# Two PSUM banks for the scores and three for the maxima in the second layer's attention, in place of three and two

## The chip, the cores and the metric

The kernel runs on one core of one Trainium2 chip. The metric is the device time of one execution in microseconds (us). Three runs of the kernel before took 1433.34, 1433.45 and 1435.84 us; their median is 1433.45 us.

## What is computed

Eight sequences of 512 tokens with 256 features go through two layers. The first is attention with 16 heads of 16 features, with rotary positions and q and k scaled to unit length. The second is an ordinary attention, without those two, followed by a mixture of eight experts, of which each token goes to the one with the largest gate. Cut to what matters here:

```python
# first layer, per sequence
q, k = unit(rope(q)), unit(rope(k))
attn = softmax(q @ k.T / 4)
x = layernorm(x + (attn @ v) @ Wo + bo)
# second layer
h = layernorm(x) * ln1_w + ln1_b
q, k, v = split(h @ w_qkv)
y = x + (softmax(q @ k.T / 4) @ v) @ w_proj
out = layernorm(x + y + expert_of_token(layernorm(y) * ln2_w + ln2_b))
```

In the first layer the scores can't exceed a small number, since q and k have unit length, so no maximum is taken off before the exponential. In the second layer they can, and each row's maximum has to be known before the exponential is taken.

## The kernel before, in words

There are 16 passes of attention: 0 to 7 for the first layer's eight sequences, 8 to 15 for the second layer's. They run as a pipeline. In one stage the scores of pass b are computed (it is the *attended* pass), while the next pass is *projected* (q, k and v) and the one before it *finished* (output projection, norms, routing). A stage has 16 quads of four chunks. A chunk is one head and one tile of 128 keys: its scores for all 512 queries fill one PSUM bank. "3.1" stands for chunk 1 of quad 3 of a stage. A stage is called by its attended pass.

TensorE (PE) issues everything in an order written out in the source: for every chunk the score matmul (`score`, L450), then, in the second layer, one max tile (`max_score`, L482), after chunk 1 of the quad the four value products of an earlier quad (`pv`, L467), and then whatever the tables PROJECTED, ATTENDED and FINISHED place at that chunk (`task`). L511 are projections of q and k, L525 those of v, L555 the output projection, L533, L548, L501 and L563 transposes, L540 the transposition of the negated maxima.

A max tile is the same product of q and k with the queries on the partitions: 128 queries of one head by 512 keys. VectorE (DVE) takes the maximum of each row, negated (`max_tile`, L868). When a group of four heads has its 16 tiles, `neg_split` (L873) splits the negated maxima into three bf16 parts; PE transposes them (L540), ScalarE (ACT) copies them (L727) and issues a DMA (L732) that puts them as three more rows into the stack of q. The score matmul of the second layer thus subtracts the maximum by itself: it has 99 rows in place of 96. The max tiles run six quads ahead of the scores (MAX_LEAD = 6): from quad 10 of a stage they are those of the next pass. So maxima appear from quad 10 of pass 7 to quad 9 of pass 15.

ACT takes the exponential of each chunk (`exp`, L665), in order, and between chunks does its own tasks of the tables: L688 copies projections to bf16, L681 copies transposed inputs, L674 the finished value products, L741 and L713 other copies, L749 and L753 the reciprocal deviation of a norm, for which it waits for DVE's moments (L968, L972). DMAs issued by ACT stand in its order too.

PSUM has eight banks of 128 x 512 fp32. Bank 4 is for projections, bank 5 (in the first layer also bank 7) for outputs, bank 6 for value products. In passes 0 to 6 the scores have banks 0 to 3. From pass 7 on, before the change, they have banks 0 to 2, and the max tiles banks 3 and 7. Two rules keep these apart. `st_bank` (L362) gives a score its bank and the count of exponentials that must be done before it may be written; with three banks that is the exponential of three chunks earlier. `mx_ring` (L348 to L360) counts, for each max bank, the reduces that have read it; `max_score` waits until its bank's last use has been reduced, with two banks that of two tiles earlier.

```python
wait(pe, exps, read)                       # score: the bank has been read
wait(pe, *mx_ring.free(b, (g, c)))         # max_score: the bank has been reduced
```

Of the kernel before, what the change touches and what calls it, by code (L numbers as in the profile page):

```python
# [25 lines left out]
CHUNKS = QUADS * HEADS_AT_ONCE  # L26
# [23 lines left out]
LAST_A = BATCH - 1  # L50
# [98 lines left out]
def program(nc, x, w_qkv1, w_o1, b_o, ln1_w, ln1_b, w_qkv2, w_o2, ln2_w, ln2_b, gate_w, gate_b,  # L149
# [5 lines left out]
    with ctx:  # L155
# [22 lines left out]
        psum = [ctx.enter_context(nc.psum_tensor(f"bank{i}", [P, T], FP32)) for i in range(8)]  # L178
# [163 lines left out]
        N_FIRST, N_LATER, N_CONST_OPS = 7, 12, 4  # L342


        st_banks, mx_banks, pv_bank = psum[0:4], (psum[3], psum[7]), psum[6]
        p_ring = Ring("proj", [psum[4]], sem)
        o_ring = Ring("out", [psum[5], psum[7]], sem)
        mx_ring = Ring("max", mx_banks, sem)  # L348
# [8 lines left out]
        for b in range(BATCH, 2 * BATCH):  # L357
            for g in range(GROUPS):
                for c in range(HEADS_AT_ONCE * TT):
                    mx_ring.add(b, (g, c), c % 2)  # L360

        def st_bank(b, c):  # L362

            if b < LAST_A:
                return st_banks[c % 4], CHUNKS * b + c - 3
            return st_banks[(CHUNKS * (b - LAST_A) + c) % 3], CHUNKS * b + c - 2

        def tiles(ap, b):
            return ap[b].rearrange("(t p) d -> p t d", p=P)
# [64 lines left out]
        def _(pe):  # L434
# [3 lines left out]
            def score(b, c):  # L438

                q, j = c // HEADS_AT_ONCE, c % HEADS_AT_ONCE  # L440
                g, kt = q // TT, q % TT
                rows = STACK + (NEG if second(b) else 0)
                if c == 0:
                    for arrived in stack_in:
                        pe.wait_ge(arrived, 16 * STACK_DMAS * (b + 1))
                if second(b) and j == 0 and kt == 0:
                    pe.wait_ge(neg_in, 16 * GROUPS * (b - BATCH) + 16 * (g + 1))
                bank, read = st_bank(b, c)
                wait(pe, exps, read)
                nc.tensor.matmul(bank[:, :],  # L450
                                 k_stack[0:rows, b % 2, HEADS_AT_ONCE * g + j,
                                         kt * P:(kt + 1) * P],
                                 q_stack[0:rows, b % 2, HEADS_AT_ONCE * g + j, :],
                                 start=True, stop=True).then_inc(scores, 1)
# [202 lines left out]
        def _(act):  # L657
            nc.scalar.preload_act_table_set("natural_log_exp_and_others")

            def exp(b, c):  # L660
                q, j = c // HEADS_AT_ONCE, c % HEADS_AT_ONCE
                act.wait_ge(scores, CHUNKS * b + (c + 1))
                if j == 0:
                    wait(act, pv_done, QUADS * b + q + 1 - PROBS)
                nc.scalar.activation(probs[:, q % PROBS, j, :], st_bank(b, c)[0][:, :],  # L665
                                     ACT.Exp, scale=SCALE).then_inc(exps, 1)
# [178 lines left out]
        def _(dve):  # L845
# [27 lines left out]
            def neg_split(b, g):  # L873

                last_tile = HEADS_AT_ONCE * TT - 1
                dve.wait_ge(*mx_ring.empty(b, (g, last_tile - 1)))
                dve.wait_ge(*mx_ring.empty(b, (g, last_tile)))
                if g:
                    dve.wait_ge(*o_ring.full(b, f"NG{g - 1}"))
                elif b > BATCH:  # L880
                    dve.wait_ge(*o_ring.full(b - 1, f"NG{GROUPS - 1}"))
                n = 3 * GROUPS * (b - BATCH)
                ve.tensor_copy(neg_parts[:, :, 0, :], negm[:, :, :]).then_inc(neg_step, 1)
                dve.wait_ge(neg_step, n + (3 * g + 1))
                ve.tensor_tensor(neg_rest[:, :, :], negm[:, :, :], neg_parts[:, :, 0, :],
                                 ALU.subtract).then_inc(neg_step, 1)
                dve.wait_ge(neg_step, n + (3 * g + 2))
                ve.tensor_copy(neg_parts[:, :, 1, :], neg_rest[:, :, :]).then_inc(neg_step, 1)
                dve.wait_ge(neg_step, n + (3 * g + 3))
                ve.tensor_tensor(neg_parts[:, :, 2, :], neg_rest[:, :, :], neg_parts[:, :, 1, :],  # L890
                                 ALU.subtract).then_inc(neg_ready, 1)
# [188 lines left out]
            for n in range(-1, STAGES + 1):  # L1080
                if n == 1:
                    dve.wait_ge(later_in, 16 * N_LATER)
                    ve.tensor_copy(earlier_bf[:, :], route_c[:, 0:P])
                    ve.tensor_copy(next_row[:, :], room_c)
                    ve.tensor_copy(token[:, :], tok_c)
                    dve.wait_ge(padded, 16 * (E + 1))
                for q in range(QUADS):
                    for b, g in split_group(n, q):
                        neg_split(b, g)
                    largest = max_tiles(n, q)  # L1090
                    for j in range(HEADS_AT_ONCE):
                        for tile in largest[j:j + 1]:
                            max_tile(*tile)
                        for name, b in tasks(n, q, j, DVE_LAG):
                            task(name, b)
# [300 lines left out]
```

## Time and profile before

| what | value |
|---|---|
| time, median of three runs | 1433.45 us |
| time of the profiled execution | 1429.04 us |
| its span, first to last instruction | 1427.1 us |
| PE matmuls busy | 90% of the span |
| DVE, ACT, GpSimd busy | 55%, 64%, 22% |
| mean granted TensorE clock | 0.966 |

Matmuls are pipelined and their ends are modelled, so a busy PE is not a PE at its peak; the distance between the starts of two matmuls tells more. "PEld" is the load of weights into PE, which can run ahead of the matmul before it. In a timeline a row has its start, its length, engine, line and operation, what it writes and reads, how many of them follow one another (x5), and in brackets the idle time of the engine before it and what ended that. Instructions on ACT and DVE overlap a little at their ends. "ACTq" is a DMA issued by ACT.

### The profile page before, as it was taken

How to read it: one execution, taken by the hardware profiler on the slowest of the kernel's cores; microseconds unless marked ns; L12 is line 12 of the kernel's file. 1: busy time of each engine (PE TensorE's matmuls, PEld its weight loads, DVE VectorE, ACT ScalarE, POOL GpSimd, SP SyncE). 2: the span in 40 equal slices, each digit the busy share in tenths (PEclk: the TensorE clock that was granted, in tenths of full speed). 3: DMA queues.
4: the chain of work that ended last, by engine and by line, in shares of the span. 5: the costliest groups of instructions: out<-in, count | busy, mean ns of one | idle time of the engine just before them, and what ended most of it. 6: DMA issues, size and time to landing. Idle time of an engine off the chain costs nothing. (4 is left out here: it accounts for less than half of the span.)

```text
span 1427.1 us, 21029 instructions
## 1 busy us (share of the span) xinstructions
PE 1279.5 (90%) x7238; PEld 687.5 (48%) x7238; DVE 792.0 (55%) x1815; ACT 919.6 (64%) x1617; POOL 311.5 (22%) x247
## 2 busy tenths in 40 slices
PE   3599999999999898999999999999961899999993
PEld 1233443443443333444434443444331898989993
DVE  3333554554552677787878787878823333433341
ACT  0277777777777565676666666766640477767773
POOL 5122233233232110222222222212122011111111
PEclk9799999999999999999999999999995899999997
DMA  7231331331432121214131313131357111111113
GB/s 194 88 99 46 127 114 56 127 114 55 127 114 92 57 90 60 81 54 104 46 104 47 105 46 109 51 96 61 134 183 244 53 49 53 56 54 52 52 56 133
DMA packets 103496, 127.87 MB, mean 90 GB/s; under 512 B 7168, under 2 KB 91008, under 8 KB 103264
## 3 DMA queue, kind: packets, MB, share of 16 engines
q1 hardware_dynamic: 71088, 79.06, 17.6%
q10 hardware_dynamic: 27872, 33.95, 7.5%
q0 software_dynamic: 4432, 13.52, 3.1%
q8 instruction: 60, 0.98, 0.3%
q14 instruction: 44, 0.36, 0.1%
HBM read 51.51 MB, written 28.46 MB: 56 GB/s over the span
## 5 line engine op out<-in xcount | busy, mean ns | idle before, releaser
L665 ACT ACTIVATE w_space<-bank 128x512 f32<-128x512 f32 x1024 | 564.4, 601 | 288.3 <-PE bank L450 275.4
L868 DVE TENSOR_REDUCE negm<-bank 128x1 f32<-128x512 f32 x512 | 334.3, 685 | 97.2 <-PE bank L482 93.6
L450 PE MATMUL bank<-w_space 96*128 96x512 bf16 (+1 forms) x1024 | 354.7, 385 | 12.4 <-DMA w_space<-work_space 9.8
L467 PE MATMUL bank<-w_space 128*32 128x512 f32 x2048 | 275.2, 610 | 0.6 <-ACT w_space L674 0.6
L450 PEld LDWEIGHTS bank<-w_space 96*128 96x128 bf16 (+1 forms) x1024 | 93.6, 99 | 278.2 <-ACT w_space L665 204.3
L482 PE MATMUL bank<-w_space 96*128 96x512 bf16 x512 | 197.3, 385 | 16.4 <-DVE negm L868 7.6
L638 PE MATMUL bank<-w_space,work_space 128*128 x624 | 141.4, 380 | 0.0
L511 PE MATMUL bank<-work_space,wqkv_sb 128*128 128x512 f32 x256 | 123.0, 603 | 7.5 <-DVE w_space L995 4.8
L638 PEld LDWEIGHTS bank<-w_space,work_space 128*128 128x128 f32 x624 | 115.5, 190 | 14.2
L1222 POOL TENSOR_TENSOR work_space<-w_space,work_space 128x1024 bf16<-128x1024 f32 x32 | 68.3, 2136 | 226.1 <-ACT work_space L713 145.7
L1278 POOL DMA_INDIRECT out_rows<-rows_sb,work_space x39 | 37.5, 963 | 267.6 <-DVE rows_sb L1172 267.6
L482 PEld LDWEIGHTS bank<-w_space 96*128 96x128 bf16 x512 | 50.1, 98 | 90.9 <-DVE negm L868 50.2
L467 PEld LDWEIGHTS bank<-w_space 128*32 128x32 f32 x2048 | 40.6, 108 | 99.5 <-issue 75.7
L1256 POOL TENSOR_TENSOR row_sb<-row_sb,rows_sb 128x512 f32<-128x512 f32 x32 | 38.0, 1187 | 207.8 <-DVE row_sb L976 207.8
L625 PEld LDWEIGHTS bank<-work_space 128*128 128x128 f32 x640 | 76.5, 196 | 1.9 <-DVE work_space L1145 0.9
L625 PE MATMUL bank<-work_space 128*128 128x128 f32 x640 | 76.8, 279 | 0.5 <-DVE work_space L1145 0.5
L1158 DVE TENSOR_TENSOR wqkv_sb<-bank,work_space 128x256 f32<-128x256 f32 x39 | 16.6, 425 | 104.7 <-PE bank L638 104.7
L511 PEld LDWEIGHTS bank<-work_space,wqkv_sb 128*128 128x128 f32 x256 | 48.2, 192 | 49.4 <-issue 31.4
L625 PEld LDWEIGHTS bank<-work_space,wqkv_sb 128*128 128x128 f32 x608 | 70.8, 192 | 1.7 <-DVE work_space L1145 0.8
L625 PE MATMUL bank<-work_space,wqkv_sb 128*128 128x128 f32 x608 | 71.1, 275 | 0.5 <-DVE work_space L1145 0.5
L525 PE MATMUL bank<-wqkv_sb,work_space 128*128 128x256 f32 x256 | 62.5, 388 | 2.5 <-DVE w_space L1008 1.7
L555 PE MATMUL bank<-wo_sb,w_space 128*128 128x256 f32 x256 | 60.8, 380 | 2.5 <-ACT w_space L741 1.6
(131 smaller groups left out, 1451.5 us busy)
## 6 DMA issues: line engine op xcount, KB each, us to landing
w_space<-work_space SPq DMA_DIRECT2D x384, 128.0 KB
w_space<-in_w_dram ACTq DMA_DIRECT2D x16, 1024.0 KB, 8.5
work_space<-rows_dram SPq DMA_DIRECT2D x39, 256.5 KB, 2.6
work_space<-in_x_dram ACTq DMA_DIRECT2D x16, 512.0 KB, 3.8
x_dram<-xo SPq DMA_DIRECT2D x16, 256.0 KB, 3.2
h_dram<-row_sb SPq DMA_DIRECT2D x16, 256.0 KB, 2.2
work_space<-h_dram ACTq DMA_DIRECT2D x8, 512.0 KB, 3.9
work_space<-x_dram ACTq DMA_DIRECT2D x8, 512.0 KB
```

The lines of the kernel that those rows point to most:

```text
L450: nc.tensor.matmul(bank[:, :], k_stack[0:rows, b % 2, HEADS_AT_ONCE * g + j, kt * P:(kt + 1) * P], q_stack[0:rows, b % 2, HEADS_AT_ONCE * ...
L467: last = nc.tensor.matmul(pv_bank[VW * j:VW * (j + 1), :], v_aug[:, b % 2, at:at + VW], probs[:, q % PROBS, j, :], start=(kt == 0), stop=( ...
L482: nc.tensor.matmul(mx_ring.bank(b, (g, c))[:, :], q_stack[0:STACK, b % 2, h, qt * P:(qt + 1) * P], k_stack[0:STACK, b % 2, h, :], start=Tr ...
L511: last = nc.tensor.matmul(bank[:, :], wqkv_sb[:, second(b), k, c * P:(c + 1) * P], xT[:, k, :], start=(k == 0), stop=(k == KD - 1))
L525: last = nc.tensor.matmul(bank[:, j * D:(j + 1) * D], xT[:, k, tt * P:(tt + 1) * P], wqkv_sb[:, second(b), k, 2 * D:3 * D], start=(k == 0) ...
L555: last = nc.tensor.matmul(bank[:, t * D:(t + 1) * D], onT[:, u, t, k, :], wo_sb[:, second(b), k, :], start=(k == 0), stop=(k == KD - 1))
L625: last = nc.tensor.matmul(psum[2 * (j % 2) + n][:, f * P:(f + 1) * P], w1_tile[j % 2][:, k, at:at + P], xsT[:, j % 2, k, :], start=(k == 0 ...
L638: last = nc.tensor.matmul(psum[5 + j % 2][:, 0:D], hidT[:, j % 2, k, :], w2_sb[:, bass.ds(e, 1), k, :].rearrange("p a d -> p (a d)"), star ...
L665: nc.scalar.activation(probs[:, q % PROBS, j, :], st_bank(b, c)[0][:, :], ACT.Exp, scale=SCALE).then_inc(exps, 1)
L868: ve.tensor_reduce(negm[:, c % TT, c // TT:c // TT + 1], mx_ring.bank(b, (g, c))[:, :], axis=AX.X, op=ALU.max, negate=True).then_inc(mx_ri ...
L1222: pool.tensor_tensor(parts[:, qk, 2, :, :], rest[:, qk, :, :], parts[:, qk, 1, :, :], ALU.subtract).then_inc(parts_ready, 1)
L1256: pool.tensor_tensor(both, both, rows_sb[:, r:r + 1, :].to_broadcast([P, 2, D]), ALU.mult).then_inc(hw_step, 1)
```

## The change

From pass 7 on, the scores alternate between banks 0 and 1, and a score waits for the exponential of two chunks earlier. Bank 2 goes to the max tiles, which take banks 2, 3 and 7 in turn through all passes; a max tile waits for the reduce of three tiles earlier. Before the negated maxima of a group are split, DVE waits for the last use of each of the three banks in place of two.

```diff
-        st_banks, mx_banks, pv_bank = psum[0:4], (psum[3], psum[7]), psum[6]
+        st_banks, mx_banks, pv_bank = psum[0:4], (psum[2], psum[3], psum[7]), psum[6]
...
-                    mx_ring.add(b, (g, c), c % 2)
+                    mx_ring.add(b, (g, c), len(mx_ring.uses) % len(mx_banks))
...
-            return st_banks[(CHUNKS * (b - LAST_A) + c) % 3], CHUNKS * b + c - 2
+            return st_banks[c % 2], CHUNKS * b + c - 1
...
-                dve.wait_ge(*mx_ring.empty(b, (g, last_tile - 1)))
-                dve.wait_ge(*mx_ring.empty(b, (g, last_tile)))
+                for back in range(len(mx_banks)):
+                    dve.wait_ge(*mx_ring.empty(b, (g, last_tile - back)))
```

## Rows read from the trace of the kernel before

**Rows 1.** The page: span, and busy time of each engine.
```profile
span 1427.1 us, 21029 instructions
PE 1279.5 (90%) x7238; PEld 687.5 (48%) x7238; DVE 792.0 (55%) x1815; ACT 919.6 (64%) x1617; POOL 311.5 (22%) x247
```

**Rows 2.** Stretches (passes 7, 8, 9-14, 15): length, busy us (count) per engine, clock, DMA.
```profile
434.29:502.96 68.67, 58.84 (x302) 22.61 (x300) 29.43 (x70) 44.44 (x87) 11.81 (x8) 0.98 0.25 79
502.96:579.51 76.55, 71.23 (x354) 27.49 (x352) 56.41 (x123) 46.34 (x89) 11.35 (x7) 0.93 0.22 70
579.51:994.41 414.90, 407.72 (x2281) 179.14 (x2278) 329.46 (x738) 279.79 (x527) 90.75 (x79) 1.00 0.24 74
994.41:1051.20 56.79, 52.58 (x313) 19.87 (x311) 37.15 (x93) 39.16 (x77) 11.55 (x12) 1.00 0.40 140
```

**Rows 3.** Waits in passes 9 to 14: who waited for whom: total us, times, longest.
```profile
PEld bank L450 <- ACT w_space L665: 61.8, 78, 0.8
...
PEld bank L482 <- DVE negm L868: 25.6, 61, 0.7
```

**Rows 4.** Timelines of PE and ACT in pass 12, around chunk 3.1.
```profile
800.67 0.38 PE L482 MATMUL bank<-w_space 96*128 96x512 bf16 x1
800.89 0.38 PE L450 MATMUL bank<-w_space 99*128 99x512 bf16 x1
801.40 0.39 PE L482 MATMUL bank<-w_space 96*128 96x512 bf16 x1
...
800.73 0.73 ACTq L732 DMA_DIRECT2D w_space<-neg_T  x1
801.56 0.60 ACT L688 ACTIVATE work_space<-bank 128x512 bf16<-128x512 f32 x1 [0.86 <-ACT neg_T L727]
...
802.05 2.56 ACT L665 ACTIVATE w_space<-bank 128x512 f32<-128x512 f32 x5
```

**Rows 5.** The same timelines, around chunk 8.3.
```profile
826.39 0.38 PE L450 MATMUL bank<-w_space 99*128 99x512 bf16 x1
...
826.87 0.30 ACT L749 ACTIVATE rstd<-mv,eps_sb 128x4 f32<-128x4 f32 x1 [1.28 <-DVE mv L972]
...
827.31 2.76 ACT L665 ACTIVATE w_space<-bank 128x512 f32<-128x512 f32 x5
```

**Rows 6.** The same timelines, around chunk 15.1.
```profile
852.66 0.38 PE L450 MATMUL bank<-w_space 99*128 99x512 bf16 x1
853.04 0.39 PE L482 MATMUL bank<-w_space 96*128 96x512 bf16 x1
...
853.07 0.60 ACT L665 ACTIVATE w_space<-bank 128x512 f32<-128x512 f32 x1 [0.81 <-PE bank L450]
```

**Rows 7.** The same timelines, around chunk 7.0.
```profile
818.65 0.38 PE L450 MATMUL bank<-w_space 99*128 99x512 bf16 x1
819.16 0.39 PE L482 MATMUL bank<-w_space 96*128 96x512 bf16 x1
...
818.52 1.57 ACT L665 ACTIVATE w_space<-bank 128x512 f32<-128x512 f32 x3 [0.81 <-PE bank L450]
```

**Rows 8.** Timeline of PE in passes 7 and 12: two waits of other tasks.
```profile
455.29 1.98 PE L511 MATMUL bank<-work_space,wqkv_sb 128*128 128x512 f32 x4 [1.31 <-DVE w_space L1000]
...
850.45 0.39 PE L540 MATMUL bank<-ident_bf,neg_parts 128*12 128x128 bf16 x4 [0.44 <-DVE logits L1069]
```

**Rows 9.** Timelines of PE and DVE in pass 8, quads 13 and 14.
```profile
565.16 0.61 PE L482 MATMUL bank<-w_space 96*128 96x512 bf16 x1 [1.69 <-DVE negm L868]
...
568.64 0.69 DVE L868 TENSOR_REDUCE negm<-bank 128x1 f32<-128x512 f32 x1 [2.14 <-PE bank L482]
...
574.44 0.69 DVE L868 TENSOR_REDUCE negm<-bank 128x1 f32<-128x512 f32 x1 [1.51 <-PE bank L482]
```

**Rows 10.** A stretch of pass 8 (as rows 2), and PE's timeline in pass 7.
```profile
564.45:574.69 10.24, 9.53 (x34) 2.79 (x35) 6.12 (x16) 3.73 (x9) 2.21 (x2) 0.50 0.07 24
...
473.08 0.38 PE L482 MATMUL bank<-w_space 96*128 96x512 bf16 x1 [2.48 <-issue]
```

## Prediction

> **What bounds the kernel now.** I read the page first: TensorE (PE) is busy for 1279.5 of 1427.1 us [rows 1]. Its first wave, the first layer, keeps four score banks, so only passes 7 to 15 can change. The table of stretches cuts these out. The six passes 9 to 14 take 414.90 us, 69.15 each, and PE is busy for 407.72 of them at granted clock 1.00, while VectorE (DVE) has 329.46 and ScalarE (ACT) 279.79 [rows 2]. So PE sets the pace there, and a pass grows by what PE stands still, whoever causes it. The next view is the waits of these six passes. PE's weight loads wait 61 times, 25.6 us in all, for DVE to give back a bank for the maxima, and 78 times, 61.8 us, for an exponential (exp) [rows 3]. A reader must take these sums with care: a load runs ahead of the matmul before it, so part of such a wait is covered by that matmul. Hence the timeline, by starts of matmuls: score and max of one chunk are 0.22 us apart when nothing waits (800.67 to 800.89 [rows 4]); more than that is standstill. I write 3.1 for chunk 1 of quad 3 in the pass that runs from 787.14 to 856.12, one of the six; the places recur in each.
>
> **The change, part by part.**
>
> *Third max bank.* max(m) now waits for the reduce of m-3, not of m-2. The typical wait it removes is at 7.0: score at 818.65, max at 819.16 [rows 7], 0.51 apart where 0.22 would do, so 0.29 us. With 61 waits in six passes, ten a pass [rows 3], the gain is at most 10 x 0.29 = 2.9 us a pass, and nothing at least, if the score ahead of the max is late anyway.
>
> *Two score banks.* score(c) now waits until exp(c-2) has read its bank, not exp(c-3). This costs wherever ACT is busy with something else between two exps. Scores that begin today before exp(c-2) has ended stand in a few places of a pass; four of them carry nearly all of it.
>
> At 3.1 ACT first spends 0.73 us issuing the DMA of the negated maxima (from 800.73), then copies a projection (801.56), and only then runs five exps from 802.05 in 2.56 us [rows 4]. One exp is 0.60 us [rows 6]. The first of the five is exp(2.3), which ends at 802.65; score 3.1 starts at 800.89 today, so it moves by 1.76. The max behind it starts at 801.40, 0.29 later than it need; that goes. Net: **+1.47**.
>
> At 8.3 ACT sits 1.28 us for the moments (idle time in front of its row at 826.87), and exp(8.1) is the first of the five from 827.31, over at 827.91. Score 8.3 starts at 826.39 [rows 5]. Net: **+1.52**; its max waits for nothing today.
>
> At 15.1 exp(14.3) runs from 853.07 to 853.67, after another DMA issue for negated maxima; the score starts at 852.66 and its max at 853.04, 0.16 over the pace [rows 6]. Net 1.01 - 0.16 = **+0.85**.
>
> At 7.0 exp(6.2) is the first of three from 818.52, over at 819.12, and the score starts at 818.65: 0.47, less the 0.29 of its max [rows 7]. Net: **+0.18**.
>
> Quads 1, 10 and 13 are of the kind of 7.0 with a smaller lateness; I take them together at zero, the middle between losing the 0.18 of 7.0 and gaining the 0.29 of a max, each.
>
> Sum: 1.47 + 1.52 + 0.85 + 0.18 = 4.02 us a pass, **24 us in six**.
>
> Behind the waiting score stand, in PE's order, its max, the four value products of the quad and all later scores. ACT is not starved while PE waits: at 3.1 it still has exp(3.0), and exp(3.1) comes when the score is done. DVE gets its maxima later and idles. Is the delay given back later in the pass? Only where PE stands for DVE or ACT for a reason that the delay doesn't move. Pass 7 has such a place: a projection at 455.29 waits 1.31 us for DVE [rows 8] and would swallow the delay ahead of it. In the six passes the one that I find is the transposition of negated maxima at 850.45, PE idle 0.44 [rows 8]; and DVE's work ahead of it starts from PE's own maxima, so it moves along. I give nothing back.
>
> *Passes 7, 8 and 15.* Here both signs occur. In pass 8 DVE falls behind on the first layer's leftovers; a max waits until 565.16 with PE idle 1.69, after which PE runs at granted clock 0.50 (1.2 GHz) for 10.24 us, and DVE itself then runs dry for 2.14 us (before 568.64) and 1.51 us (before 574.44) [rows 9, 10]. A third bank lets PE run ahead there, so DVE needn't run dry: about 3.6 us gained, at most. Pass 7 has the same pattern, and where it has no maxima yet, late scores besides. Pass 15 has no projections but late scores to its end. Their bounds: three times the loss of a full pass, +12, and the 3.6 of pass 8 and about as much less in pass 7, -6. I take **0** for the three.
>
> *The negated maxima.* neg_split has three waits for maxima in place of two, on DVE's own reduces, of which the last still ends last: nothing, 32 waits in all.
>
> The profiled execution took 1429.04 us: 1429 + 24 = 1453. The median of the runs shown is 1433.45, 4.4 above it, so I put the forecast at 1433.45 + 24, **1457.5 us**.
>
> **The rivals.**
>
> *The clock falls.* The new standstills, 1.8 us at 3.1 and 1.5 at 8.3, come in every pass. In pass 8 PE stood 1.69 us and ran at half rate next [rows 9, 10]; such a stretch of 10.24 us costs about half of itself, 5.1 us. One in each of the six passes would add 31 us, one of a third of that length 10: 1468 to 1489, say 1480. Against it: PE stood 2.48 us before 473.08 [rows 10], and the passes 9 to 14 and that stretch show no fall. In pass 8 there were also several shorter stops just ahead. The Trainium skill, page "TensorE: Matmul & The Clock Gate", section "A second HAM failure mode: psum-queue depth-cycling", says that a TensorE which idles briefly between groups of matmuls as it cycles through PSUM banks swings between half and full clock; by that rule this rival would be the likeliest. The six passes do cycle banks with short waits at clock 1.00 [rows 2, 3], so the trace so far does not bear it out. Chance 0.15.
>
> *The third max bank wins (faster).* If the score's delay lies beside other waits, as 1.48 us could at 455.29 [rows 8], what is left is the gain on maxima: 6 x 2.9 and the 6 of passes 7 and 8, some 23 us: 1410; with half of it, 1422. It decides as soon as less of a pass's late scores reaches the end of the pass than the maxima give back. For it: the 25.6 us of waits [rows 3]. Against it: at 3.1 and 8.3 PE's work goes straight on behind the score, with no wait to lie beside. Chance 0.05.
>
> *Nothing changes.* If the exps in question were in truth over before their scores are due, or ACT's order shifted with PE's so that lateness and gain cancel, the time stays at 1433, within 3. Against it: ACT's busy stretches at 3.1 and 8.3 hang on DVE's moments and the DMA issue, not on the score. Chance 0.05.
>
> **How the numbers follow.** The forecast has 0.75. Its own ends: 6 x 3.15 (quads 1, 10 and 13 each gaining 0.29) with the edges at -6, that is +13, 1446; and 6 x 4.5 (each losing 0.18) with the edges at +12, that is +39, 1473. I reach a little into the clock's case, to 1478. Left out are most of that case and the two others, about 0.2. A measurement tells about 0.2%, 2.9 us, from no change. Faster 0.05, within 0.05, slower 0.90.
>
> **What would show it.** Right: a full pass of 73 us in place of 69.15; in each, PE idle about 1.8 us ahead of score 3.1 and 1.5 us ahead of 8.3, ended by an exp; the loads' waits for DVE's reduces near zero, those for exps well above 61.8 us; in pass 8 DVE no longer dry before 568.64 and no half clock there. Wrong: PE's idle time ahead of 3.1 unchanged; passes of 69 us or less; granted clock under 1.00 in passes 9 to 14; or a pass that grows by more than 4.5 us at clock 1.00, which would mean that ACT's own work moves behind the late scores and makes the next ones late too.

## The result, and the profile after

The changed kernel takes 1461.53 us (median of four runs, 1458.98 to 1463.29) against 1433.39 us before (four runs): slower by a ratio of 1.0188, 95% interval 1.0169 to 1.0206. The forecast was 1457.5, in a range of 1446 to 1478. The profiled execution after took 1458.98 us, 29.9 above that of before. The page's first part [rows 1]:

```profile
span 1456.9 us, 21060 instructions
...
PE 1285.8 (88%) x7238; PEld 685.7 (47%) x7238; DVE 794.9 (55%) x1815; ACT 927.1 (64%) x1617; POOL 310.9 (21%) x247
```

Every engine has the same number of these instructions as before; the 31 more in the total (21060 after 21029) are of the kinds that don't count as busy, such as waits. PE's busy time grew by 6.3 us, the span by 29.8: the loss is mostly PE standing still.

Where the time went is read from the same stretches as before, cut at the first score of each pass [rows 2]. The columns are start and end, length, busy us (and instructions) of PE, PEld, DVE, ACT and GpSimd, granted clock, DMA share and GB/s. The lines are passes 7, 8, 9 to 14 together, and of these passes 10 and 11 alone.

```profile
434.08:504.60 70.52, 61.60 (x303) 23.23 (x301) 29.42 (x70) 45.41 (x87) 11.75 (x8) 0.95 0.23 75
504.60:577.82 73.22, 67.61 (x354) 26.08 (x352) 57.20 (x123) 46.78 (x89) 11.32 (x7) 1.00 0.23 73
577.82:1022.33 444.51, 414.68 (x2281) 178.22 (x2279) 331.44 (x738) 284.90 (x527) 90.56 (x79) 0.98 0.23 69
650.91:725.64 74.73, 69.80 (x383) 30.26 (x381) 55.31 (x124) 47.61 (x89) 15.90 (x15) 0.98 0.27 72
725.64:798.73 73.09, 68.16 (x383) 29.61 (x381) 55.32 (x124) 47.61 (x89) 15.74 (x15) 1.00 0.24 73
```

Passes 9 to 14 take 444.51 us in place of 414.90, that is 29.6 more, practically the whole loss. Two of them (9 and 11) take 73.09 at granted clock 1.00, 3.94 more than the 69.15 of before. The other four take 74.3 to 74.7, each with 3.4 us at half clock. So about 6 x 3.94 = 23.6 us are standstill, and the remaining 6.0 came with the clock. The edges have both signs, as argued: pass 7 has 1.85 more, pass 8 has 3.33 less, and pass 15, from its first to its last score, takes 60.15 in place of 56.42, 3.73 more. The rest of the program has 1.9 less (29.9 - 29.6 - 1.85 + 3.33 - 3.73).

The waits of passes 9 to 14 changed places [rows 3]:

```profile
PEld bank L450 <- ACT w_space L665: 106.6, 124, 2.1
PEld bank L450 <- issue: 17.6, 33, 1.7
PEld bank L482 <- issue: 8.0, 24, 0.3
```

The 61 waits of the max loads for a reduce, 25.6 us, are gone altogether: this view has no row for them any more. The waits of the score loads for an exp rose from 61.8 to 106.6, and the longest from 0.8 to 2.1. The four places in pass 11, from the timeline of PE, each behind the matmul just before it, and (last three lines) of ACT:

```profile
738.95 0.38 PE L482 MATMUL bank<-w_space 96*128 96x512 bf16 x1
740.98 0.39 PE L450 MATMUL bank<-w_space 99*128 99x512 bf16 x1 [1.65 <-ACT w_space L665]
...
758.23 0.38 PE L482 MATMUL bank<-w_space 96*128 96x512 bf16 x1
758.97 0.39 PE L450 MATMUL bank<-w_space 99*128 99x512 bf16 x1 [0.37 <-ACT w_space L665]
...
766.18 0.38 PE L482 MATMUL bank<-w_space 96*128 96x512 bf16 x1
767.97 0.39 PE L450 MATMUL bank<-w_space 99*128 99x512 bf16 x1 [1.41 <-ACT w_space L665]
...
794.28 0.24 PE L580 MATMUL bank<-one_hot,ones_bf 128*128 128x32 bf16 x4
795.44 0.39 PE L450 MATMUL bank<-w_space 99*128 99x512 bf16 x1 [0.92 <-ACT w_space L665]
...
739.01 0.73 ACTq L732 DMA_DIRECT2D w_space<-neg_T  x1
739.84 0.60 ACT L688 ACTIVATE work_space<-bank 128x512 bf16<-128x512 f32 x1 [0.86 <-ACT neg_T L727]
740.33 1.67 ACT L665 ACTIVATE w_space<-bank 128x512 f32<-128x512 f32 x3
```

These are scores 3.1, 7.0, 8.3 and, behind four small matmuls, 15.1 [rows 4 to 7]. ACT's order at 3.1 is the old one: 0.73 us of issuing, a copy, then the exps. The first of the three, exp(2.3), ends 0.60 after 740.33; the score starts 0.05 later. By starts of matmuls, score 3.1 comes 2.03 after the max before it, 8.3 comes 1.79 after, where 0.22 would do. "Idle" in brackets is less than that, since the modelled end of the matmul before is later than the next one could start.

The half clock, in pass 10, is at the same place. The first three lines are of PE's timeline, the last of the stretches:

```profile
666.25 0.39 PE L450 MATMUL bank<-w_space 99*128 99x512 bf16 x1 [1.65 <-ACT w_space L665]
666.48 0.38 PE L482 MATMUL bank<-w_space 96*128 96x512 bf16 x1
666.79 1.57 PE L467 MATMUL bank<-w_space 128*32 128x512 f32 x8
...
667.22:670.63 3.41, 3.41 (x16) 1.53 (x9) 1.66 (x3) 0.66 (x2) 0.00 (x0) 0.50 0.71 249
```

PE stands 1.65 us ahead of score 3.1, and 0.97 us after it starts again (666.25 to 667.22) the clock falls to 1.2 GHz. In the other three passes the fall begins between 0.1 us before and 0.8 us after the start of score 3.1. The value products take 1.57 in place of 1.06. In pass 11 the same 1.65 us were followed by full clock.

In pass 8 the third bank did what was expected. DVE's row that answers to the dry spell before 568.64 [rows 9] is

```profile
567.23 3.05 DVE L868 TENSOR_REDUCE negm<-bank 128x1 f32<-128x512 f32 x5
```

Five reduces in a row, no dry spell (none from there to 575 either), and pass 8 has granted clock 1.00 where it had 0.93.

### The profile page after: what moved, and what is told of

Its sections match the earlier page's. It is cut to its first block, busy times and chain, and to the rows that moved or that the text cites. A ratio compares the mean times of both kernels' runs of the same rounds, so it can differ in the third digit from the quotient of the medians.

```text
span 1456.9 us, 21060 instructions
## 1 busy us (share of the span) xinstructions
PE 1285.8 (88%) x7238; PEld 685.7 (47%) x7238; DVE 794.9 (55%) x1815; ACT 927.1 (64%) x1617; POOL 310.9 (21%) x247
## 4 chain that ended last, share of the span: by engine, by line
PE 74%; DVE 6%; ACT 5%; DMA 5%; issue 4%; ACTq 3%; SPq 1%; POOL 1%; POOLq 0%; DVEq 0%
PE bank L450 16%; PE bank L467 15%; PE bank L511 8%; PE bank L625 8%; PE bank L638 7%; PE bank L482 6%; PE bank L555 4%; PE bank L525 4%; DVE negm L868 3%; ACT w_space L665 2%; DMA work_space<-rows_dram 2%; PE bank L518 2%; DMA out_rows<-rows_sb,work_space 2%; PE bank L533 2%; ACTq L762 1%
## 5 line engine op out<-in xcount | busy, mean ns | idle before, releaser
L665 ACT ACTIVATE w_space<-bank 128x512 f32<-128x512 f32 x1024 | 570.6, 599 | 313.5 <-PE bank L450 298.9
```

## The experiments

The theory is that PE loses what its scores wait for exps that ACT runs late, and that ACT is late where its order holds something else between two exps: the issue of a DMA, or a wait for DVE.

### The third max bank alone undone

```diff
-        st_banks, mx_banks, pv_bank = psum[0:4], (psum[2], psum[3], psum[7]), psum[6]
+        st_banks, mx_banks, pv_bank = psum[0:4], (psum[3], psum[7]), psum[6]
```

> Scores keep two banks, the maxima go back to two (banks 3 and 7; bank 2 lies idle): the third max bank alone is undone. Theory (late scores): the loss is that of the scores, so it stays, and the waits for max banks come back where the score ahead is not late anyway: a full pass of 73.4 to 74.0 us where the clock stays up, passes 7 and 8 lose again what the third bank gave them (pass 8 about 76 us or more, with a stretch of half clock); 1464 to 1475 us. Rival (the third max bank does the harm, because PE runs ahead and pushes its work in front of others): a full pass back near 69 us, 1433 to 1440 us.

Measured: 1474.07 us, ratio 1.0289 (1.0251 to 1.0328). A full pass took 73.41 us, in five of six at full clock, and pass 8 took 75.7. Stretches of the profile, pass 9, pass 8, and the half clock in pass 7:

```profile
585.53:658.94 73.41, 68.50 (x383) 29.85 (x381) 55.36 (x124) 47.62 (x89) 11.67 (x9) 1.00 0.19 60
509.80:585.53 75.73, 67.82 (x354) 26.48 (x352) 57.49 (x123) 46.88 (x89) 11.33 (x7) 1.00 0.21 69
493.20:503.40 10.20, 9.02 (x31) 2.13 (x32) 6.29 (x17) 3.20 (x9) 1.76 (x2) 0.50 0.08 26
```

The loss stays without the third max bank, so the scores' lost bank is its cause. The third max bank is worth only 73.41 - 73.09 = 0.32 us in a full pass, and 2.5 us in pass 8, which has full clock in both profiles. The time itself doesn't price that bank: of the 8.8 us that this profile is longer than that of the changed kernel, 4.4 lie in passes 7 and 8, 1.6 in pass 15, and 5.7 ahead of pass 7 and behind the last score, while passes 9 to 14 have 2.9 less. The half clock moved from pass 8 to pass 7 here; pass 8 kept full clock in this execution, which I had not expected.

### The DMA of the negated maxima off ACT

```diff
...
                     act.wait_ge(*o.empty(b, name))
-                    act.dma_start(q_stack[STACK:STACK + NEG, b % 2,
-                                          HEADS_AT_ONCE * u:HEADS_AT_ONCE * (u + 1), :],
-                                  neg_T[:, :]).then_inc(neg_in, 16)
...
+                elif kind == "NG":
+                    sp.wait_ge(*o_ring.empty(b, name))
+                    sp.dma_start(q_stack[STACK:STACK + NEG, b % 2,
+                                         HEADS_AT_ONCE * u:HEADS_AT_ONCE * (u + 1), :],
+                                 neg_T[:, :]).then_inc(neg_in, 16)
```

The first part is ACT's task NG, whose wait goes with the issue; the second is SyncE's order, at the place of the same task.

> The changed kernel, with the DMA of the negated maxima issued by SyncE in place of ScalarE. Theory (late scores, because ScalarE is held up between two exps): the 0.73 us of the issue goes at three places, so PE stands 1.1 us in place of 1.8 ahead of 3.1, 0.2 in place of 0.9 ahead of 15.1, nothing in place of 0.5 ahead of 7.0: a full pass of 71.2 us in place of 73.1, and with the shorter standstills no more half clock in passes 9 to 14 (it cost about 1.6 us in each of four of them); 1443 to 1450 us. Rival 1 (ScalarE's copies hold it, and the issue runs beside them): 73 us a pass, 1458 to 1463 us. Rival 2 (the clock falls for another reason): 71.2 us a pass, but still half clock in some; 1448 to 1454 us.

Measured: 1447.73 us, ratio 1.0088 (1.0061 to 1.0115). Score 3.1 in pass 11, ACT ahead of it, and passes 9 to 14:

```profile
733.90 0.39 PE L450 MATMUL bank<-w_space 99*128 99x512 bf16 x1 [0.66 <-ACT w_space L665]
...
732.30 0.59 ACT L727 ACTIVATE neg_T<-bank 12x512 bf16<-12x512 bf16 x1
732.80 0.57 ACT L688 ACTIVATE work_space<-bank 128x512 bf16<-128x512 f32 x1
733.27 1.65 ACT L665 ACTIVATE w_space<-bank 128x512 f32<-128x512 f32 x3
...
577.87:1002.49 424.62, 408.27 (x2279) 176.53 (x2279) 330.43 (x738) 282.15 (x526) 90.62 (x79) 1.00 0.25 73
```

ACT's copies now follow one another without the gap, and PE's idle time ahead of 3.1 fell from 1.65 to 0.66. A full pass takes 70.84, so 2.25 less than 73.09, at full clock throughout. Theory right, and the issue with its wait costs a little more than the 0.73 us of the issue: by starts of matmuls, standstill fell by 0.99 us at 3.1, 0.34 at 7.0 and 0.93 at 15.1, together the 2.25. But pass 15 grew from 60.15 to 67.71 us, from its first to its last score: PE waited 3.41 us there for the last group's maxima, and 13.7 us of it ran at half clock.

```profile
1055.67 1.04 PE L450 MATMUL bank<-w_space 99*128 99x512 bf16 x2 [3.41 <-DMA w_space<-neg_T]
...
1048.22 0.37 ACTq L758 DMA_DIRECT2D w_space<-in_w_dram  x1
1048.62 0.61 ACTq L758 DMA_DIRECT2D w_space<-in_w_dram  x1
1049.03 0.70 SPq L1317 DMA_DIRECT2D w_space<-neg_T  x1
```

ACT, freed of its wait, issued two expert weights of 1 MB each ahead of the 12 KB that PE needed; in the changed kernel, the order on ACT itself had put the small one first.

### R2 two chunks later on ACT

```diff
-NG1=0, TP0=2, R2=3,
+NG1=0, TP0=2, R2=5,
```

> The changed kernel, with the second layer's R2 (ScalarE's two instructions that wait for VectorE's moments) two chunks later in ScalarE's order. Theory: exp(8.1) no longer stands behind that wait, PE's standstill of 1.57 us ahead of 8.3 goes in seven passes: a full pass of 71.5 to 71.7 us in place of 73.1; 1449 to 1454 us. Rival (ScalarE or VectorE comes late next: the norm that waits for R2 delays VectorE's reduces, and a max waits for them): a wait of the max's load at quad 9 in its place, 1457 us or more.

Measured: 1455.27 us, ratio 1.0133 (1.0109 to 1.0158); 6 us less than the changed kernel, but 1.3 above the 1449 to 1454 of the theory; the kernel before took 1435.15 in this comparison, 1.8 more than in the first. In passes 9 to 14 the theory is right to the tenth: four of six take 71.51 or 71.52 (the others 72.10 and 71.08), and score 8.3 comes 0.22 after the max before it, as if nothing waited. R2 at 835.71 has no idle time in front of it any more. Pass 12, PE first, then ACT:

```profile
834.99 0.38 PE L482 MATMUL bank<-w_space 96*128 96x512 bf16 x1
835.21 0.38 PE L450 MATMUL bank<-w_space 99*128 99x512 bf16 x1
...
835.71 0.30 ACT L749 ACTIVATE rstd<-mv,eps_sb 128x4 f32<-128x4 f32 x1
...
1008.56:1077.00 68.44, 62.91 (x314) 22.46 (x312) 37.13 (x93) 40.81 (x78) 12.72 (x14) 0.83 0.33 116
1054.40:1078.30 23.90, 23.38 (x91) 8.06 (x88) 2.96 (x17) 12.02 (x22) 2.38 (x4) 0.50 0.32 101
```

The last two lines are pass 15, and in it 23.9 us at half clock: it gave part of the gain back. Score 3.1 still had its 1.65 us in every pass here, and no pass from 9 to 14 saw half clock.

### Both moves

> The changed kernel with both: negated maxima's DMA issued by SyncE, R2 two chunks later. Theory: both gains add, a full pass of 69.5 to 70.0 us with only 3.1 still standing about 1.1 us; no half clock in passes 9 to 14; pass 8 keeps its 73 us: 1431 to 1438 us, within 0.3% of the kernel before. Rival (two score banks bind elsewhere as soon as these places are cleared, so that the gains do not add): 1442 us or more.

Measured: 1439.44 us, ratio 1.0032 (1.0014 to 1.0049), 1.4 above the expected range; the profiled execution is the fastest of ten, 1432.94. The gains in passes 9 to 14 add:

```profile
574.08:990.06 415.98, 407.45 (x2278) 177.02 (x2279) 329.38 (x738) 281.68 (x526) 90.74 (x79) 1.00 0.25 74
990.06:1055.00 64.94, 55.45 (x319) 20.25 (x320) 37.19 (x94) 40.48 (x78) 11.89 (x13) 0.95 0.34 123
```

Passes 9 to 14 take 415.98, 1.1 more than before. What is missing is pass 15 with its late DMA, for which PE waits 3.36 us here, and 6.8 us of half clock: 64.07 us from first to last score, where the kernel before has 56.42.

### Both moves, but in the last pass ACT issues

The edits of the two runs above, with `b < 2 * BATCH - 1` as a condition for SyncE and the old lines on ACT for the rest.

> The changed kernel with both moves, but in the last pass ScalarE issues the DMA of the negated maxima as it did (with SyncE as issuer it went out behind 2 MB of expert weights there, and PE waited 3.4 us for it). Theory: full passes 69.3 us as with both moved, pass 15 at 60 us in place of 64; 1427 to 1435 us, the same as the kernel before within 0.3%. Rival (pass 15 is long because its many short standstills bring the clock down, whoever issues the DMA): pass 15 at 62 us or more with half clock in it, 1433 to 1440 us.

Measured: 1434.42 us, ratio 0.9985 (0.9974 to 0.9995), and pass 15 back at 59.4 us from first to last score, 60.41 in the row. Passes 9 to 14, pass 15, and a line of PE's timeline in pass 14:

```profile
576.05:995.59 419.54, 408.69 (x2278) 177.19 (x2279) 329.88 (x739) 281.74 (x526) 91.24 (x80) 1.00 0.25 74
995.59:1056.00 60.41, 53.82 (x319) 20.11 (x320) 37.23 (x94) 40.70 (x78) 11.36 (x13) 1.00 0.39 132
...
991.27 0.61 PE L450 MATMUL bank<-w_space 99*128 99x512 bf16 x1 [1.75 <-ACT w_space L665]
```

Passes 9 to 14 take 3.6 us more than with both moves, most of it in pass 14, which takes 71.84 in place of 68.82. There ACT issues again for the maxima of pass 15, score 15.1 waits 1.75 us, and 3.4 us of half clock go with it. So with two banks for the scores the kernel is no slower than before, once ACT's two hold-ups lie elsewhere. It is not level pass by pass: against the profile of before, passes 9 to 14 have 4.6 us and pass 15 has 3.0 more here, and pass 8, with its third max bank, has 4.2 less.

### The control: both moves with three score banks

> The control: the kernel before (three score banks, two max banks) with R2 two chunks later, and with the DMA of the negated maxima on SyncE in all passes but the last. Theory: with three score banks no score waits for those hold-ups of ScalarE, so there is nothing to win: full passes of 69.0 to 69.2 us, 1431 to 1437 us. Rival (the two moves are good whatever the banks, and the gains seen with two score banks say nothing of them): full passes of 67.5 us or less, 1425 us or less.

Measured: 1435.97 us, ratio 0.9993 (0.9984 to 1.0002); passes 9 to 14:

```profile
587.72:1001.65 413.93, 407.58 (x2280) 179.06 (x2278) 329.58 (x739) 279.52 (x527) 90.77 (x79) 1.00 0.25 74
```

68.99 us a pass, as before. The same two moves that save 3.8 us a full pass with two score banks save next to nothing with three. The hold-ups were there all along; the third score bank covered them.

### Banks shared out by pass

Passes 7 and 8, where DVE is behind, gain from the third max bank (1.9 and 2.5 us, from the run that undid it); passes 9 to 15 lose from the two score banks. So each gets its own.

```diff
+        AHEAD = HEADS_AT_ONCE * (QUADS - MAX_LEAD)
+        MX3 = CHUNKS + HEADS_AT_ONCE * (MAX_LEAD - 1)
...
-                    mx_ring.add(b, (g, c), len(mx_ring.uses) % len(mx_banks))
+                    n = len(mx_ring.uses)
+                    mx_ring.add(b, (g, c), n % 3 if n < MX3 else 1 + n % 2)
...
-            if b < LAST_A:
+            if b < LAST_A or (b == LAST_A and c < AHEAD):
                 return st_banks[c % 4], CHUNKS * b + c - 3
-            return st_banks[c % 2], CHUNKS * b + c - 1
+            if b <= BATCH:
+                return st_banks[c % 2], CHUNKS * b + c - 1
+            if b == 2 * BATCH - 1 and c >= AHEAD:
+                return st_banks[(3, 0, 1, 2)[(c - AHEAD) % 4]], CHUNKS * b + c - 3
+            return st_banks[(2, 0, 1)[(CHUNKS * (b - BATCH - 1) + c) % 3]], CHUNKS * b + c - 2
```

(The first score on a bank that was a max bank waits for its last reduce, and the first max tile for the exps up to AHEAD.)

> Banks shared out by pass: four for the scores in pass 7 until its first max tile (quad 10), then two for the scores and three for the maxima to the end of pass 8, then three and two as before, and four again in pass 15 when the maxima are done. Theory: passes 9 to 14 as before (69.1 us, no half clock), pass 8 as in the changed kernel (73.2, in place of 76.55) with no stretch of 10 us at half clock, pass 7 at 66.5 to 68.5 in place of 68.68; 3 to 6 us less than before: 1427 to 1432 us. Rival (what passes 7 and 8 gain is given back at once, since the next pass or the end waits for something else, or the clock falls elsewhere): 1433 to 1437 us.

Measured: 1430.30 us against 1436.82 of the kernel before in the same comparison, ratio 0.9952 (0.9939 to 0.9964). Faster as expected, by 0.5%, but not by the expected way: pass 8 took 75.91, not 73.2, and pass 7 took 69.49, not 66.5 to 68.5. The profiles don't show where the gain lies: from pass 7 to the last score of pass 15 this one takes 616.0 us and that of the kernel before 616.5, but the latter is of an execution of 1429.04 us, faster than any of the 23 of this comparison (1434.68 at least). The granted clock of the runs, 0.965 in the median against 0.962, would make some 4 us of it, an estimate from 0.003 of 1430 us. Up to quad 15 it ran like the changed kernel (quad 15 begins 68.30 us after its start in both). There the max tiles had two banks again (L493 is the max here), and PE stood:

```profile
574.80 0.45 PE L493 MATMUL bank<-w_space 96*128 96x512 bf16 x1 [0.94 <-DVE negm L879]
575.18 1.94 PE L478 MATMUL bank<-w_space 128*32 128x512 f32 x8
```

### The third max bank kept to the end of pass 8

```diff
-        MX3 = CHUNKS + HEADS_AT_ONCE * (MAX_LEAD - 1)
+        MX3 = CHUNKS + HEADS_AT_ONCE * MAX_LEAD
```

> Banks by pass again, but the third max bank is kept to the very end of pass 8 (the version before gave it back one quad earlier: its quad 15 took 7.6 us in place of 4.9, with a max that waited 1.3 us and half clock from then on). Theory: pass 8 at 73.2 to 73.6 us in place of 75.9, passes 9 to 14 unchanged at 69 to 69.3; 2 to 3 us less than that version: 1426 to 1430 us on the same footing as 1430.3. Rival (the first score of pass 9 now waits for the last reduce of the bank that it takes over, and loses as much): pass 8 at 75 us or more, 1429 to 1433 us.

> The same with both moves (R2 two chunks later; the DMA of the negated maxima on SyncE but for the last pass). Theory: pass 8 at 72.2 to 72.6 us in place of 74.8; 1424 to 1429 us. Rival: the moves bring nothing on top, the time is that of the version without them.

Measured: 1429.14 us, ratio 0.9957 (0.9940 to 0.9974), and with both moves 1427.94 us, ratio 0.9947 (0.9932 to 0.9961). Pass 8 without and with the moves, and passes 9 to 14 with them:

```profile
505.63:579.44 73.81, 67.77 (x355) 26.04 (x353) 57.63 (x123) 47.08 (x89) 11.33 (x7) 1.00 0.23 73
```

```profile
504.81:577.44 72.63, 67.70 (x353) 26.15 (x353) 57.13 (x123) 46.51 (x88) 11.34 (x7) 1.00 0.23 74
577.44:991.60 414.16, 407.60 (x2279) 179.07 (x2279) 329.36 (x738) 279.06 (x526) 90.62 (x79) 1.00 0.26 75
```

Pass 8 came out nearly as the theory has it, 2.1 and 2.2 us less than with the bank given back early (75.91, and 74.84 with the moves). In the time the step is too small to show: the ratios 0.9952, 0.9957 and 0.9947 overlap, as does 0.9941 (0.9926 to 0.9956) of the next run. All of them beat both kernels, the one before by 0.4 to 0.6%.

### Banks by pass, given back early, with both moves

> Banks by pass, and both moves (R2 two chunks later; the DMA of the negated maxima on SyncE but for the last pass). Theory: the moves shorten only passes with two score banks, so pass 8 goes from 73.2 to about 72.2, pass 7 by up to 1 us, passes 9 to 14 stay at 69.1; 1425 to 1431 us. Rival (the moves bring nothing on top, or hold SyncE's queue up in pass 8): as the kernel with banks by pass alone, or slower.

Measured: 1429.10 us, ratio 0.9941 (0.9926 to 0.9956); pass 8 took 74.84, not 72.2, for the reason just seen. The moves bring no gain in time that can be told from the version without them.

## Why the prediction was right

**What sets the pace.** Right. A pass grew by what PE stands still, and at full clock by nothing else; the time grew by the six passes.

**The four places.** Right, each by name and nearly by size. Standstill against the prediction's lateness: 3.1 1.81 (2.03 less 0.22) for 1.76, 8.3 1.57 for 1.52, each 0.05 more, since a score starts that much after the exp ends; 7.0 0.53 (0.75 less 0.22) for 0.47; 15.1 1.06 for 1.01 (it starts 1.16 after the four small matmuls of 794.28, where it was 0.10). Together that is 4.97 of standstill for the 4.76 of the sum. Net of the vanished waits for max banks, a pass at full clock grew by 3.94, for 4.02 predicted; the closeness of the net is in part luck, as the next point shows. That ACT's order causes it is shown from both sides: taking the DMA issue out removed 2.25 us a pass, putting R2 later 1.57, both together 3.76 (73.09 less 415.98 / 6) of the 3.94, and both together only 0.16 with three score banks (69.15 less 68.99).

**The third max bank.** The price was rightly small, at 0.32 us a pass, within the bounds of nothing and 2.9. The waits that it removes stand mostly behind scores that are late anyway. But the 0.74 that the sum takes off at 3.1, 7.0 and 15.1 is not its doing: with two max banks, too, the max follows 0.23 after the late score at these places. There a full pass grew by 4.26 (73.41 less 69.15), which is the 4.97 less 0.71 of such waits. The third bank's own 0.32 comes from places that the sum put at zero. Two small misses, 0.2 too little standstill and 0.3 too little gain, cancel.

**Nothing given back.** Right for the six passes: the 4.26 just worked out is the four standstills less the max waits behind them, with nothing left over.

**The edges.** Taken at 0, they came to +2.3 in the profile (1.85 - 3.33 + 3.73): near it, but only because 3.33 and 3.73 happen to cancel; nothing in the sum made them do so. The lower bound of -6 is a little short of its own terms, since 3.6 twice is 7.2. The mechanism in pass 8 is shown by what it lost without the third max bank (75.73 in place of 73.22) and where that bank was given back early (75.91 in place of 73.81).

**The clock.** This is the term that the forecast left out and the rival over-priced. Four of six passes fell to half clock for 3.4 us and grew by 1.2 to 1.6 each, 6.0 in all; the rival's lowest case was six at 1.7. It is as large as the distance from 24 to the 29.9 of the profile. Granted clock under 1.00 in passes 9 to 14 was one of the prediction's own signs of being wrong, and it came (0.98): the rival's fall happened, beside the forecast's standstill and not in place of it, and the range was wide enough for both. The trace of before had shown both outcomes, a stop with a fall behind it and a longer one without [rows 9, 10], and so it is among the runs: the same 1.65 us ahead of 3.1 brought half clock in four passes of six here, in one of six without the third max bank, and in none of six with R2 later. What decides stays open. The Trainium skill, page "TensorE: Matmul & The Clock Gate", section "A second HAM failure mode: psum-queue depth-cycling", has the clock swing when TensorE idles briefly between groups of matmuls as it cycles through PSUM banks. The four passes agree with that, with 3.4 us at clock 0.50 in each; the passes that kept full clock show that it need not happen.

**The other rivals.** That the third max bank wins fell with the run that undid it: slower, not faster. That nothing changes fell with the result.

## What to carry to other kernels

Here the number of banks that the scores need is set not by ACT's mean rate but by the longest stretch in which ACT does something else between two exps. In another kernel, look for DMA issues and waits in the consumer's own order between two reads, and compare their length with what the remaining banks cover. A buffer that covers a hold-up can be had back by moving the hold-up, and a move that saves nothing today may pay once the buffer goes. Where phases of a program need different splits, the split can change with the phase.

## What the runs showed that I had not expected

Removing a wait from one queue reordered DMAs on another: with the small DMA on SyncE, two transfers of 1 MB went out 0.8 us and 0.4 us ahead of it, and 12 KB took PE 3.41 us of waiting.

Pass 15, where many short waits for exps follow one another, has half clock in some profiles and not in others: none in the changed kernel's profile (60.15 us from first to last score), 23.9 us of it with R2 later (67.5). Within one kernel the time spreads accordingly more than before: 1467.67 to 1483.75 without the third max bank, where the kernel before kept within 1431.81 to 1437.61. The granted clock of the single runs agrees: without the third max bank 1467.67 us has 0.965, the two of 1474 have 0.961, and 1483.75 has 0.950; with both moves the fastest of ten, 1432.94, has 0.967 and the slowest, 1445.69, has 0.958. Within the kernel before, where both spread little, the clock doesn't order the times.
